# Products with the values ahead of the shifted scores in TensorE's step

## The reference

```python
# third layer (adjacency as a weight), one graph, head h
logits = q @ k.T / sqrt(32) + log(clip(adj, 1e-8))
out = softmax(logits) @ v            # then @ Wo + bo, residual, layer norm
# fourth layer
logits = q @ k.T / sqrt(32) + (2 * adj - 1)
w = softmax(logits) * (0.25 + 0.75 * adj)
w = w / max(sum(w), 1e-6)
out = w @ v                          # then @ Wo, residual, layer norm, feed-forward
```

## Time and profile before

| | |
|---|---|
| median of three executions | 4511.79 us (4506.36 to 4515.14) |
| the profiled execution | 4507.2 us, its span 4505.4 us |
| PE (TensorE) busy | 4099.7 us, 91% |
| DVE (VectorE) | 3033.0 us, 67% |
| ACT (ScalarE) | 2211.1 us, 49% |
| POOL (GpSimd) | 1924.4 us, 43% |
| mean granted TensorE clock | 0.955 |

### The profile page before, as it was taken

The page is one execution under the profiler, slowest core; times in us unless marked ns, Lnnn a source line. Parts: engine busy times, 40 slices in busy tenths (PEclk is TensorE's granted clock), DMA queues, the critical chain, the costliest instruction groups (busy, mean ns, idle before and its releaser), DMA issues.

```text
span 4505.4 us, 69471 instructions
## 1 busy us (share of the span) xinstructions
PE 4099.7 (91%) x21040; PEld 2192.1 (49%) x21040; DVE 3033.0 (67%) x5152; ACT 2211.1 (49%) x3894; POOL 1924.4 (43%) x1064
## 2 busy tenths in 40 slices
PE   7998999989999899998999989998999989999898
PEld 6534365344753447543474434744347443564334
DVE  3687737877378764787647876478755787557774
ACT  3365533655336553465534655246543465435663
POOL 1174701746027560265503655036540465404563
PEclk9998999999999999999999999999999999999999
DMA  3201102011020110201102011120111101111010
GB/s 106 75 18 32 52 17 70 18 34 50 25 62 17 34 50 30 59 15 36 48 30 59 15 36 49 33 57 13 38 50 34 52 13 39 52 36 50 10 41 15
DMA packets 106289, 176.57 MB, mean 39 GB/s; under 512 B 27296, under 2 KB 50336, under 8 KB 105888
## 3 DMA queue, kind: packets, MB, share of 16 engines
q1 hardware_dynamic: 105888, 171.69, 13.3%
HBM read 83.12 MB, written 8.39 MB: 20 GB/s over the span
## 4 chain that ended last, share of the span: by engine, by line
PE 56%; issue 17%; POOL 14%; DVE 7%; ACT 3%; SPq 2%; DMA 1%; POOLq 0%; DVEq 0%; ACTq 0%
POOL region_p L1446 11%; PE ps L706 9%; PE ps L573 9%; PE ps L565 9%; PE ps L625 8%; PE ps L675 7%; PE ps L654 6%; PE ps L792 4%; PE ps L614 2%; DVE region_p L1181 2%; POOL rstd L1456 1%; SPq L475 1%; DMA region_k<-region_p 1%; POOL y_t L1515 1%; SPq L399 1%
## 5 line engine op out<-in xcount | busy, mean ns | idle before, releaser
L1446 POOL TENSOR_TENSOR region_p<-region_p,mask 128x1024 f32<-128x1024 f32 x608 | 1444.8, 2390 | 489.9 <-ACT region_p L920 488.9
L1195 DVE TENSOR_REDUCE row_max_bf<-ps 128x1 bf16<-128x1024 f32 x768 | 939.7, 1224 | 197.2 <-PE ps L675 184.9
L706 PE MATMUL ps<-region_p,shelf 128*64 128x512 f32 x3584 | 949.7, 600 | 5.1 <-ACT o_raw L943 5.1
L920 ACT ACTIVATE region_p<-ps 128x512 f32<-128x512 f32 x1216 | 664.2, 596 | 349.0 <-PE ps L654 346.8
L654 PE MATMUL ps<-region_q,region_k 97*64 97x512 bf16 x4096 | 715.3, 401 | 24.2 <-DVE region_p L1181 15.3
L675 PE MATMUL ps<-region_k,region_q 96*64 96x512 bf16 x3584 | 593.7, 399 | 7.8 <-DVE row_max_bf L1191 7.8
L1181 DVE TENSOR_TENSOR region_p<-ps,mask 128x512 f32<-128x512 f32 x832 | 529.7, 680 | 76.4 <-ACT ps L916 76.1
L916 ACT ACTIVATE ps<-ps 128x512 f32<-128x512 f32 x832 | 445.9, 580 | 260.4 <-PE ps L654 254.4
L1456 POOL TENSOR_TENSOR rstd<-var_eps,minus_half 128x2 f32<-128x2 f32 (+1 forms) x160 | 116.9, 730 | 972.2 <-DVE var_eps L1127 972.2
L654 PEld LDWEIGHTS ps<-region_q,region_k 97*64 97x64 bf16 x4096 | 255.0, 112 | 463.7 <-DVE region_p L1181 195.5
L675 PEld LDWEIGHTS ps<-region_k,region_q 96*64 96x64 bf16 x3584 | 200.8, 113 | 428.4 <-issue 385.7
(11 more groups left out here) (160 smaller groups left out, 5342.0 us busy)
## 6 DMA issues: line engine op xcount, KB each, us to landing
mask<-in_adj SPq DMA_DIRECT2D x64, 512.0 KB, 7.4
mask<-in_adj_t SPq DMA_DIRECT2D x64, 512.0 KB, 3.4
y_t<-o_raw SPq DMA_DIRECT2D x224, 64.0 KB, 2.0
sums_t<-o_raw SPq DMA_DIRECT2D x224, 64.0 KB, 2.0
region_q<-region_p SPq DMA_DIRECT2D x192, 64.0 KB, 2.0
region_k<-region_p SPq DMA_DIRECT2D x192, 64.0 KB, 2.0
region_q<-sums_t SPq DMA_DIRECT2D x192, 64.0 KB, 2.0
region_k<-sums_t SPq DMA_DIRECT2D x192, 64.0 KB, 2.0
```

The source lines that it names most:

```text
L706: last = nc.tensor.matmul(ps[64 * c:64 * c + 64, VALUE_BANK, :], values_and_one, probs[:, t % RING, c * HALF:(c + 1) * HALF], start=(t == ...
L920: nc.scalar.activation(probs[:, t % RING, c * HALF:(c + 1) * HALF], scores_t, ACT.Exp, scale=DK ** -0.5).then_inc(exp_done, 1)
L1195: nc.vector.tensor_reduce(row_max_bf[i][:, t:t + 1], flat[:, (t % 2) * N:(t % 2 + 1) * N], AX.X, ALU.max)\
L1446: nc.gpsimd.tensor_tensor(p, p, mask[:, t, :], ALU.mult).then_inc(masked_pool, 1)
```

## The change

In TensorE's `head` the call of `with_values` moves from behind the shifted scores to ahead of them. A step was maxima's products, shifted scores, products with the values; it becomes maxima's products, products with the values, shifted scores. No instruction is added or taken away, and the other engines' lists stay as they are.

```diff
                     if h < H - 2:
                         scores_for_maximum(b, layer, (0, h + 2), t)
+                    if t >= LAG:
+                        with_values(b, layer, h, t - LAG)
+                    elif h:
+                        with_values(b, layer, h - 1, T - LAG + t)
                     if t == 0:
                         pe.wait_ge(max_row_in[h % 2], max_rows_in(b, layer, (0, h + 2), h % 2))
                     for c in range(2):
...
                         last.then_inc(st_done, 1)
-                    if t >= LAG:
-                        with_values(b, layer, h, t - LAG)
-                    elif h:
-                        with_values(b, layer, h - 1, T - LAG + t)
```

## The result

The changed kernel takes 4635.11 us (median; 4634.57 to 4639.12). In the runs taken beside it the kernel before took 4510.31 us, so it is 124.8 us slower: ratio 1.0277, 95% interval 1.0265 to 1.0289. The prediction was 4625, with 4578 to 4672 as its range and 0.93 on slower.

A forecast was written before the change was run, and what follows sets the result against it. TensorE, busy 91% of the span, was taken to set steady heads of 15.05 us. Added waits of 106 us and 8 for the clock on 4507.2 gave 4621 profiled, 4625 forecast as median, range 4578 to 4672.

The forecast's parts named there:

- The banks: Steady heads: scores ask for their PSUM banks 0.86 us later, so waits fall from 0.82 to 0.31 us a head.
- The copy: Tile 0's values in step 3 wait for ScalarE's copy: +0.85 us in heads 1 to 5, 1.7 us waits in heads 6, 7.
- GpSimd in heads 6 and 7: Masked tiles need 4.1 us, the new order leaves 3.0: +3.0 us in layer 1, +2.7 in layer 0.
- The sum: All waits won and made: +7.0 us in layer 1, +6.3 in layer 0, +106 us for eight graphs.
- The clock: TensorE's clock drops after long waits in the tail heads: +8 us taken, bounds 0 and 54.
- only the copy: Rival: only the copy's wait is real, GpSimd's chain has more slack; 4570 us, chance 0.14.
- faster: Rival: banks' gain comes, ScalarE's copy causes no new wait; 4462 us if GpSimd's wait falls away too, chance 0.04.
- no change: Rival: waits won and made cancel, or the order of matmuls has no effect; 4505 to 4520 us, chance 0.03.
- The swing of the clock: Rival: a slow stretch a head; 4672 us if in heads 6 and 7 alone, 4836 in all 128 heads, chance 0.15.

The follow-up runs named there:

- the early copy: Changed kernel with ScalarE's copy of the finished head moved ahead of tile 2's exponentials, in all heads: 4524.18 us, ratio 1.0033 to the kernel before.
- half-length multiplication: Changed kernel with GpSimd multiplying only 512 of 1024 columns with the mask in heads 6 and 7: 4599.1 us, ratio 1.0190 to the kernel before.
- the run of heads 6 and 7: New order in heads 6 and 7 only, old order in heads 0 to 5: 4610.51 us, ratio 1.0215 to the kernel before.

## Why the prediction was right, and where its terms were off

*The banks.* Predicted -0.51 us a head. The prediction found 0.82 us of such waits in a steady head before. After, the scores take 0.43 us in steps 5 and 7, and 0.20 is left in step 2 where 0.31 was to be left. So the gain is about 0.6. The table of waits, which leaves out the shortest, has the same: first before, then after.

```profile
PE ps L654 <- DVE region_p L1181: 15.3, 80, 0.2
```

```profile
PE ps L658 <- DVE region_p L1181: 0.6, 2, 0.4
```

The steady heads of 14.72 us with the early copy, 0.33 under the old 15.05, show a gain of its own, for at most 0.14 of it can be the copy's old wait.

*The copy.* Right, and shown by the run with the early copy. In heads 1 to 5 the wait was to be 1.0 to 1.1 us and is 1.14. The prediction's own terms give 2.3 - 1.17 = 1.13. It put down +0.85 for the change and measured is 1.14 - 0.14 = +1.00. Banks and copy together were to cost a steady head 0.34 and cost 0.42: both terms were a little small, and the errors have opposite signs. In head 6 the wait was to be 1.7 us and is 1.70. But the 0.33 that was taken off it is the profile's printed idle time, while the 1.7 counts from starts. By starts it was 0.50 before, so the change is +1.2 and not +1.4. In head 7 of layer 1 it went from 0.86 to 1.70, +0.8 where +1.1 was put down. In layer 0 of the third graph it went from 2.3 to 2.7, +0.4 where +0.7 was put down.

*GpSimd in heads 6 and 7.* Right. From the scores to the masked tile 4.1 us were predicted, 4.05 measured. By starts, in layer 1 of the second graph, TensorE waits 1.09 and 0.97 us for tiles 3 and 7 of head 6, and 0.38, 0.77 and 0.36 for tiles 3, 4 and 6 of head 7. Two of them, as the profile prints them:

```profile
1103.76 1.08 PE L706 MATMUL ps<-region_p,shelf 128*64 128x512 f32 x4 [0.80 <-POOL region_p L1446]
...
1114.14 1.06 PE L699 MATMUL ps<-region_p,shelf 128*32 128x512 f32 x8 [0.70 <-POOL region_p L1446]
```

That makes 3.6 us where 3.4 were predicted, and 0.5 was lost at these places before: +3.1 against +3.0. In layer 0 of the third graph it is +2.9 against +2.7. The half-length multiplication gives back less, 29 us of the 46 predicted, since it uncovers waits for VectorE (22.3 us in L699). So 29 is what a shorter chain would win, and no measure of the term. The claim that the steady heads keep 0.2 to 0.3 us to spare held only because of the copy's hole, as the run with the early copy shows.

*The sum.* In layer 1 +7.0 us was predicted, and from the first scores to the last values of the second graph it is 125.4 - 117.6 = 7.8. By parts and over the same matmuls, head 0 lost 0.2 (it was to win 0.51), heads 1 to 5 lost 1.9 (2.0), head 6 lost 2.6 and head 7 with the rest 3.1 (5.5 together). So the sum came out by its parts, and only head 0 is off. There the granted clock is 0.78 before and 0.76 after, and the prediction put it down like a steady head; what held it up is not shown. In layer 0 +6.3 was predicted. It is 128.9 - 121.4 = 7.5 in the third graph. There head 0 won 0.5, heads 1 to 5 lost 1.9, and head 6 and head 7 with the rest lost 6.2, where 4.8 were predicted for these two. The second graph has 127.7 - 121.4 = 6.3, but that it fits is luck: its tail lost as much, and head 0, at a granted clock of 0.91 instead of 0.75, made up for it. What the tail lost beyond the prediction goes with the clock in head 7 with the rest. Its windows over the same matmuls, third graph, before and after:

```profile
1432.67:1451.55 18.88, 16.20 (x111) 5.00 (x108) 14.10 (x16) 14.91 (x24) 13.77 (x6) 0.91 0.06 15
```

```profile
1469.15:1491.69 22.54, 17.79 (x111) 3.74 (x110) 14.79 (x16) 15.77 (x25) 12.57 (x5) 0.85 0.05 12
```

By these clocks 3.4 us more of the stage lie at the lower level, which can cost at most 1.7.

Over all eight graphs layer 0 lost 57 us and layer 1 62, where 50 and 56 were predicted. Another 1.6 us were lost behind layer 0 of the second graph, up to layer 1's first scores, which the sum had at nothing. Here too the instructions are the same and the clock is lower (second graph, before and after):

```profile
894.50:968.84 74.34, 56.68 (x247) 33.22 (x240) 50.03 (x107) 38.55 (x73) 22.15 (x25) 0.93 0.14 34
```

```profile
917.50:993.46 75.96, 58.62 (x247) 33.81 (x240) 50.11 (x108) 38.57 (x73) 22.18 (x25) 0.89 0.14 33
```

By these clocks 6 us more of the stage lie at the lower level, which can cost at most 3. That is enough for the 1.6, but no run shows that the clock alone makes them.

*The clock.* Predicted +8 us of at most 54. The lower level is half the upper one, so from the mean granted clock (1 - 0.950) x 2 x 4633.3 = 463 us of the span after lie at the lower level, and (1 - 0.955) x 2 x 4505.4 = 405 before. The 58 us more did half the work, so at most 29 us were lost in them. The two windows of head 7 above give a price: 2.8 us were lost where 0.17 x 2 x 20.55 = 7.0 us were at the lower level. At that price the 58 us cost about 23, an estimate, and less where a slow stretch lies under a wait. The direction was right; 8 was probably too small, and no run settles the size.

The rivals: "only the copy" fell with the half multiplication and with the run of heads 6 and 7; "faster" and "no change" fell with the result. The swing of the clock is true to a part. The Trainium skill's rule that I weighed (page "TensorE: Matmul & The Clock Gate", section "A second HAM failure mode: psum-queue depth-cycling") would, as I carried it over, have the clock swing in all heads with small gaps. In the four steady heads after, with 1.14 us of gap in each 15.46, the granted clock is 1.00, so for them the trace does not bear it out. In head 7, which has waits of 1.7 us and more and shorter ones behind, the clock falls at times: in layer 1 of one of eight graphs after, and of three in the run of heads 6 and 7.

## What to carry to other kernels

Where an engine runs at 90% of its time, moving a block in its step changes no work, but it changes how long every result has until it is asked for; write that down for each consumer, before and after, and look for the one whose slack turns negative. Look too at the queue of the engine that serves the moved block: here most of the loss, 110 of 125 us, came from ScalarE's order having been made for the other one. With the copy moved along the steady heads gain, and the whole is a gain once heads 6 and 7 keep the old order. Where steps differ (a last head without its prefetch, a pair of tiles on the slow engine), choose the order step by step; the version with the new order in four steps of eight is 0.9% faster than the kernel before.

## What the runs showed of the hardware

The same stage of the same kernel takes 2.8 us longer where part of it runs at the lower clock level (17.79 and 20.55 us above). Head 0 shows it in the changed kernel: in layer 0 of the second graph it takes 14.65 us, in layer 0 of the third 16.00 (windows of the kernel after):

```profile
790.48:805.13 14.65, 14.10 (x91) 5.55 (x89) 13.06 (x15) 8.82 (x17) 9.44 (x5) 0.91 0.17 42
1362.76:1378.76 16.00, 16.00 (x93) 5.94 (x89) 13.11 (x15) 8.82 (x17) 9.50 (x5) 0.77 0.16 39
```

At the clock of 0.77 TensorE counts as busy all the time, though it does no more: a full busy share can mean slow matmuls. So heads are to be compared at the same granted clock and over the same count of matmuls, or a change of a few us in a stage is read as something that it isn't.
